# Scores in four row groups per batch, one PSUM ring of seven banks, maxima moved by halves, and a new order of steps, in a two-block transformer kernel

## The reference

```
per attention:  xn = layernorm(x) (* (1 + scale) + shift)
                q, k, v = xn or context @ weights (+ bias)        # second block: rotary on q and k
                attn = softmax(q @ k.T / sqrt(8)) @ v             # 16 heads
                x = x + (gate *) (attn @ W_o + b_o)
per MLP:        x = x + (gate *) (gelu(norm(x) @ W1 + b1) @ W2 + b2)
```

## Time and profile before

| what | value |
| --- | --- |
| median of 3 runs (lowest to highest) | 484.12 us (484.04 to 486.06) |
| the profiled execution | 484.91 us |
| its span in the profile | 483.0 us |
| mean granted TensorE clock | 0.954 of full |
| PE busy | 409.0 us (85%) |
| DVE busy | 327.5 us (68%) |
| ACT busy | 268.2 us (56%) |
| POOL busy | 160.4 us (33%) |
| chain that ended last | PE 57%, DVE 15%, ACT 11%, issue 7%, POOL 7% |

### The profile page before, as it was taken

One profiled execution on the slowest core, in us unless ns is written; L12 is line 12 of the kernel. 1 busy time (PEld: TensorE's weight loads), 2 busy tenths in 40 slices (PEclk: granted clock), 3 DMA queues, 4 the chain that ended last, 5 costly groups with the idle time before them and its releaser, 6 DMA issues.

```text
span 483.0 us, 10203 instructions
## 1 busy us (share of the span) xinstructions
PE 409.0 (85%) x3872; PEld 252.5 (52%) x3872; DVE 327.5 (68%) x842; ACT 268.2 (56%) x505; POOL 160.4 (33%) x147
## 2 busy tenths in 40 slices
PE   3595869697989879889889799789899999998696
PEld 2343445464656544454454454465565655657464
DVE  5484757759597873783874875899999998431331
ACT  1211645465556647546556566556666667677452
POOL 6728515151616160160160160153251634020130
PEclk9856999989899999999999999999999999999899
DMA  8933021120312120300300400303123030400001
GB/s 249 324 97 123 12 91 45 63 73 24 107 41 92 61 71 4 103 28 2 131 3 2 132 5 0 132 6 130 57 76 108 25 128 4 142 12 24 2 1 43
DMA packets 19399, 33.52 MB, mean 69 GB/s; under 512 B 3871, under 2 KB 8479, under 8 KB 19103
## 3 DMA queue, kind: packets, MB, share of 16 engines
q1 hardware_dynamic: 18903, 32.79, 20.8%
q10 hardware_dynamic: 448, 0.08, 0.1%
HBM read 6.51 MB, written 1.05 MB: 16 GB/s over the span
## 4 chain that ended last, share of the span: by engine, by line
PE 57%; DVE 15%; ACT 11%; issue 7%; POOL 7%; SPq 2%; DMA 1%; ACTq 0%; DVEq 0%; POOLq 0%
PE ps_ao L1025 9%; PE ps_sc L1008 7%; PE ps_misc L916 7%; PE ps_misc L964 7%; DVE maxima L711 6%; PE ps_misc L1052 5%; PE ps_misc L1073 5%; PE ps_misc L986 4%; ACT PT L885 4%; POOL Kd L790 4%; PE ps_misc L921 4%; PE ps_misc L1059 3%; ACT xnT L871 3%; PE ps_misc L973 2%; PE ps_misc L1034 2%
## 5 line engine op out<-in xcount | busy, mean ns | idle before, releaser
L885 ACT ACTIVATE PT<-ps_sc 128x512 f32<-128x512 f32 (+1 forms) x256 | 138.8, 596 | 95.1 <-PE ps_sc L1008 94.4
L711 DVE TENSOR_REDUCE maxima<-ps_misc 128x4 f32<-128x512 f32 (+1 forms) x256 | 154.1, 666 | 33.0 <-PE ps_misc L986 32.8
L790 POOL TENSOR_SCALAR Kd<-Kh,head_rows 128x512 fp32r<-128x512 f32 (+1 forms) x64 | 100.3, 1582 | 132.0 <-ACT Kh L843 79.1
L1008 PE MATMUL ps_sc<-Qd,Ks 64*128 64x256 f32 (+1 forms) x512 | 64.7, 331 | 20.6 <-ACT PT L885 12.2
L1025 PE MATMUL ps_ao<-PT,V 120*18 120x128 f32 (+1 forms) x2048 | 71.8, 281 | 2.8 <-ACT PT L885 2.7
L1008 PEld LDWEIGHTS ps_sc<-Qd,Ks 64*128 64x128 f32 (+1 forms) x512 | 37.8, 183 | 57.2 <-issue 34.2
L771 POOL TENSOR_SCALAR vareps<-mv 128x4 f32<-128x4 f32 (+1 forms) x28 | 6.7, 240 | 168.2 <-DVE mv L605 167.6
L1025 PEld LDWEIGHTS ps_ao<-PT,V 120*18 120x18 f32 (+1 forms) x2048 | 51.3, 99 | 17.9 <-issue 6.2
L916 PE MATMUL ps_misc<-cst 128*128 128x384 f32 x128 | 55.8, 552 | 1.8 <-DVE att L725 1.6
L986 PE MATMUL ps_misc<-Kd,Qh 32*128 32x512 f32 (+1 forms) x256 | 44.9, 522 | 12.6 <-POOL Kd L790 8.3
L871 ACT ACTIVATE xnT<-ps_misc,vec 128x128 f32<-128x128 f32 x80 | 30.1, 457 | 40.6 <-PE ps_misc L921 40.6
(11 more groups left out here) (80 smaller groups left out, 474.7 us busy)
## 6 DMA issues: line engine op xcount, KB each, us to landing
Qd<-Qh SPq DMA_DIRECT2D x64, 128.0 KB, 2.6
Qd<-Ql SPq DMA_DIRECT2D x32, 128.0 KB, 2.6
Ks<-Kh SPq DMA_DIRECT2D x32, 128.0 KB, 2.6
Ks<-Kh SPq DMA_DIRECT2D x32, 120.0 KB, 2.6
Ks<-Kl SPq DMA_DIRECT2D x16, 128.0 KB, 2.6
Ks<-Kl SPq DMA_DIRECT2D x16, 120.0 KB, 2.6
W<-weights SPq DMA_DIRECT2D x1, 1792.0 KB, 16.8
x<-x_in SPq DMA_DIRECT2D x4, 256.0 KB, 5.9
```

Of the source, the lines that this page charges most:

```text
L711: dve.tensor_reduce(maxima[:, c, :, st.b], bank(st.use + c)[:, 0:NG * ns].rearrange("p (n k) -> p n k", n=NG), AX_X, ALU.max, negate=True) ...
L790: pool.tensor_scalar(Kd[:, st.f % 2, st.h, 0:n], f32(Kh[:, st.f % 2, 0:n]), head_rows[:, st.h:st.h + 1], None, ALU.mult).then_inc(S["kd_re ...
L885: act.activation(PT[0:ns, st.k % PSLOTS, g, :, :, :].rearrange("p i e t -> p (i e t)"), ps_sc[0:ns, g, :], ACT.Exp, scale=SCALE).then_inc( ...
L1008: ins = pe.matmul(ps_sc[0:ns, side, i * E * P:(i + 1) * E * P], Ks[rows, st.f % 2, n, st.b * ns:(st.b + 1) * ns], Qd[rows, st.f % 2, :, n, ...
```

## The change

What it does, part by part:

- A `score` step is one batch. Each of 16 matmuls has 32 rows and 128 columns; four consecutive ones go to the four row groups and to four banks. `Qd` loses its dimension of two and with it the zero halves; each key or query move is one DMA of 256 KB in place of two of 128 KB.
- `ps_sc` is gone. Scores use four banks of the one ring, which has seven. ScalarE takes four exponentials per step. `PT` holds three batches in place of four half batches.
- The maxima are transposed, copied and moved in two halves of two batches; the first scores wait for the first half only. `values` of two batches fill `ps_ao` before a `copy`, as before in number.
- `warm` matmuls stand in front of `norm` and `aT` (one each, 384 columns), and no longer in front of `xT`, `o`, `h2`, `yT`.
- ScalarE issues the loads of the context, its transpose, the second part of the weights and the bias rows, after its first exponential. The two norms' statistics have semaphores of their own.
- The formula of times is replaced by a table with one pair of times (for `plan` and for `late`) for every step of every unit.

```diff
-BANKS = 5
+BANKS = 7
-PSLOTS = 4
-WARM = {"xT": 2, "o": 1, "h2": 1, "yT": 1}
+PSLOTS = 3
+WARM = {"norm": 3, "aT": 3}
...
-T = dict(
...
-EARLY = [-0.01, -3.59, -1.1, 0.07]
-MLP_LATER = {6: 11.9}
+TIMES = {
...
+    "max": ((23.57, 24.98, 27.38, 30.38, 32.77, 46.21, 50.26, 53.8, 61.91, 67.66, 69.68, 73.68, 83.46, 89.21,
...
+    "score": ((35.18, 36.51, 39.03, 41.28, 57.78, 59.84, 63.84, 65.65, 79.13, 81.39, 85.39, 87.2, 100.68, 102.97,
...
+    "mT": ((29.18, 33.98, 50.74, 58.28, 71.17, 79.63, 92.72, 101.18, 113.88, 121.9, 135.2, 140.25, 153.17,
...
+        elif st.kind == "mods":
+            uses.append(("vec_ready", NV))
+        elif st.kind == "score":
+            uses += [("probs_ready", HG * st.k + c + 1) for c in range(HG)]
...
-        Qd = sb("Qd", [P, 2, E, NG, CT], F32R)
+        Qd = sb("Qd", [P, 2, NG, CT], F32R)
-        maxima = sb("maxima", [P, HG, NG, CB])
-        maxT = sb("maxT", [H * CB, P], F32R)
-        PT = sb("PT", [P, PSLOTS, GP, GP, E, P])
+        maxima = sb("maxima", [P, 2, HB, HG, NG])
+        maxT = sb("maxT", [H * HB, 2, P], F32R)
+        PT = sb("PT", [P, PSLOTS, HG, NG, P])
...
-        ps_sc = ctx.enter_context(nc.psum_tensor("ps_sc", [P, 2, CT], F32))
...
                         for part in (0, 1) if high else (2,):
-                            for e in range(E):
-                                sp.dma_start(f32(Ks[ROW * e + part:P:E * ROW, st.f % 2, :, 0:n]),
-                                             f32(src[HALF * e:HALF * (e + 1), st.f % 2, 0:n])
-                                             ).then_inc(S[f"keys_in{st.f % 2}"], 16)
+                            sp.dma_start(f32(Ks[part:P:ROW, st.f % 2, :, 0:n]),
+                                         f32(src[:, st.f % 2, 0:n])).then_inc(S[f"keys_in{st.f % 2}"], 16)
...
+                        for b in range(HB):
+                            at = (HB * st.h + b) * P
+                            sp.dma_start(f32(Qd[SPLIT:P:TROWS, st.f % 2, :, at:at + P]),
+                                         f32(maxT[H * b:H * (b + 1), st.h, :])
+                                         ).then_inc(S[f"maxima_in{st.f % 2}_{st.h}"], 16)
...
+                act.wait_ge(S["small_in"], 48)
+                act.activation(silu[:, 0, :], condT, ACT.Exp, scale=-1.0).then_inc(S["exp_done"], 1)
                 for c in range(HG):
                     act.dma_start(bias_qk[TROWS * c:TROWS * c + TROWS, :],
                                   by_rows(biases[:, BIAS["q0"]:BIAS["k1"] + 1], c)).then_inc(S["bias_in"], 16)
+                act.dma_start(craw[0:NS_CTX, :, :, :].rearrange("p s b f -> p (s b f)"),
+                              ctx_in).then_inc(S["ctx_in"], 16)
+                act.dma_start(W[:, W_SECOND - W_FIRST:W_TOTAL - W_FIRST],
+                              weights[:, W_SECOND:W_TOTAL]).then_inc(S["rest_in"], 16)
...
                     elif st.kind == "score":
...
-                        for g in range(GP):
-                            act.wait_ge(S[f"scores_ready{g}"], st.k + 1)
-                            act.activation(PT[0:ns, st.k % PSLOTS, g, :, :, :].rearrange("p i e t -> p (i e t)"),
-                                           ps_sc[0:ns, g, :], ACT.Exp, scale=SCALE).then_inc(S["probs_ready"], 1)
+                        act.wait_ge(S["misc_filled"], st.use + HG)
+                        for c in range(HG):
+                            act.activation(PT[0:ns, st.k % PSLOTS, c, :, :].rearrange("p n t -> p (n t)"),
+                                           bank(st.use + c)[0:ns, :], ACT.Exp,
+                                           scale=SCALE).then_inc(S["probs_ready"], 1)
...
-                        for i in range(GP):
-                            n = GP * st.g + i
-                            for side in range(GP):
-                                rows = slice(HALF * side, HALF * (side + 1))
-                                ins = pe.matmul(ps_sc[0:ns, side, i * E * P:(i + 1) * E * P],
+                        if st.b % HB == 0:
+                            pe.wait_ge(S[f"maxima_in{st.f % 2}_{st.b // HB}"], 16 * HB * (st.f // 2 + 1))
+                        for n in range(NG):
+                            for c in range(HG):
+                                rows = slice(TROWS * c, TROWS * c + TROWS)
+                                if n == 0:
+                                    fill(st.use + c)
+                                ins = pe.matmul(bank(st.use + c)[0:ns, n * P:(n + 1) * P],
                                                 Ks[rows, st.f % 2, n, st.b * ns:(st.b + 1) * ns],
-                                                Qd[rows, st.f % 2, :, n, st.b * P:(st.b + 1) * P],
+                                                Qd[rows, st.f % 2, n, st.b * P:(st.b + 1) * P],
                                                 start=True, stop=True)
```

More of the change, by code:

```diff
@@ L194, in make_plan, with at @@
 def make_plan():
     steps = []
[L203 to L210, removed]
+    def at(name, number, st):
+        when, late = TIMES[name]
+        steps.append((when[number], len(steps), st))
+        st.late = late[number], len(steps)
     for f in range(len(ATTN) * STREAMS):
-        a, s, t = f // STREAMS, f % STREAMS, period * f
+        a, s = f // STREAMS, f % STREAMS
@@ L223, in make_plan @@
[L223 to L230, removed]
+            at("cstats", s, Step("cstats", **who))
+            at("cln", s, Step("cln", **who))
@@ L244, in make_plan @@
-        at(t + period + T["aT"][a], Step("aT", **who))
+            at("max", CB * f + b, Step("max", b=b, **who))
+            at("score", CB * f + b, Step("score", b=b, **who))
+            at("value", CB * f + b, Step("value", b=b, **who))
+        for h in range(2):
+            for kind in ("mT", "mmove", "copy", "norm"):
+                at(kind, 2 * f + h, Step(kind, h=h, **who))
+        at("aT", f, Step("aT", **who))
         if ATTN[a]["gate"] is None:
             if ATTN[a]["bias"]:
-                at(t + T["bias"][a], Step("bias", **who))
-            at(t + period + T["o"][a], Step("out", **who))
-        else:
-            at(t + period + T["o"][a], Step("o", **who))
-            at(t + period + T["yT"][a], Step("yT", **who))
+                at("bias", s, Step("bias", **who))
+            at("out", f - STREAMS, Step("out", **who))
+        else:
+            at("o", s, Step("o", **who))
+            at("yT", s, Step("yT", **who))
@@ L270, in make_plan @@
+    at("mods", 0, Step("mods"))
     plan = [st for _, _, st in sorted(steps, key=lambda x: x[:2])]
-    rest = Step("mods")
-    rest.late = [st for st in plan if st.kind == "q" and st.f == 0][0].late
-    plan.insert([st.kind for st in plan].index("q") + 1, rest)
     for s in range(STREAMS):
@@ L445, in block_kernel, with scored @@
         GROUPS = NG * CB
-        MOVES = 16 * E * SPLIT
-        def scored(engine, pairs):
-            for g in range(GP):
-                engine.wait_ge(S[f"scores_ready{g}"], pairs)
+        MOVES = 16 * SPLIT
+        def scored(engine, units):
+            engine.wait_ge(S["probs_ready"], HG * CB * units)
         def bank(n):
@@ L913, in warm @@
                 def warm(st):
-                    for _ in range(WARM[st.kind]):
-                        pe.matmul(bank(st.use)[:, 0:3 * P], ident, ident[:, None, :].to_broadcast([P, 3, P]),
+                    n = WARM.get(st.kind, 0)
+                    if n:
+                        pe.matmul(bank(st.use)[:, 0:n * P], ident, ident[:, None, :].to_broadcast([P, n, P]),
                                   start=True, stop=True)
```

325 lines of the change are left out of this document (210 added, 115 removed), and 54 rows, old and new, of the table TIMES.

## The result

The changed kernel takes 449.61 us (median of four runs, 447.26 to 450.05) against 484.21 us (484.04 to 486.06). The ratio of the two is 0.926, 95% interval 0.923 to 0.929: 34.6 us less. On another chip the same kernel took 449.33 us, ratio 0.925 (0.921 to 0.929). 449.61 us is inside the stated range of 418 to 456 and outside the likeliest case's own range of 421 to 442: between the forecast of 431 and the rival of the coupled ring, 461.

A forecast was written before the change was run, and what follows sets the result against it. PE with its waits was taken as the bound, with DVE in D and chains of short steps in the front and F. Gains of front and stretches summed to 42.5 to 63.7, taken as 54: 484.9 - 54 = 431 us, range 418 to 456.

The forecast's parts named there:

- the rival of the coupled ring: Scores and maxima share one ring, so in-order PE waits for VectorE and densities fall five points: 461 us, 17 in 100.
- Scores in four row groups: Score steps on PE: a batch takes 0.44 us, saving 0.43 a batch, 27.5 us over 64 batches.
- Ring: Shared PSUM banks: a score may wait behind a reduction; costed from no gain in PE's busy share to 0.914.
- My own sign of being wrong: Wrong if PE waits on reductions or exponentials before filling banks for more than some 20 us in all.
- Warming: Matmuls on PE that keep the clock up: 48 in place of 64, 14.0 us less PE work.
- A: Stretch from 46.0 to 144.6 us before, scores of units 0 to 3: gain 11.2 to 18.7 us.
- the clock rival: The granted clock falls and PE's work at 1.2 GHz takes twice as long, 60 us more: 491 us, 4 in 100.
- Front: Start of the kernel, 0 to 46.0 us before: first score at 35.5, 10.5 us earlier, bounds 8 and 12.
- B and C: Stretches 144.6 to 200.0 and to 303.3 us before, units 4 to 8: gains 7.2 to 8.5 and 13.8 to 17.2 us.
- D and E: Stretches 303.3 to 390.0 and to 440.1 us before, units 9 to 14: gains 0 to 2.2 and 1.3 to 2.1 us.
- F: Last stretch, after 440.1 us before, a chain from x through statistics to MLP: gain 1 to 3 us.
- Moves, halves, and ScalarE's loads: Key and query transfers, maxima by halves and ScalarE's load issues: moves covered, loads and halved zeroing taken as 0.

The follow-up runs named there:

- the cut of the maxima: The changed kernel with each maxima reduction reading only half of its columns and the exponentials' scale cut to an eighth: 429.77 us, ratio 0.887.
- doubled scores: The changed kernel with the 16 score matmuls of every batch issued twice: about 471 us, ratio to before 0.9716.
- six banks: The changed kernel with six banks in the ring instead of seven, the order of steps not placed anew: 480.29 us, ratio 0.988.
- half exponentials: The changed kernel with each exponential taking half of its columns, the other probabilities staying at one: 432.16 us, ratio 0.890.

## Why the prediction came out as it did

Right in sign and within the range; too optimistic by 18.6 us in the likeliest case. Point by point:

- **What bounds the kernel**: right for TensorE (four fifths of added work show), but incomplete. Half the columns of the maxima gave 12.5 us in the kernel before, and I had read VectorE's 0.57 to 0.75 of busy time as room everywhere but in D. A page of shares doesn't show this. The waits of TensorE's loads for reductions do: 9.8 us before, 16.5 after. My sum also took PE's busy time as work, and the cut of the maxima took 15 us off it without taking a matmul away.
- **Scores in four row groups**: the mechanism is right (loads side by side), the size is not. A batch takes 0.57 and not 0.44 us of TensorE. Over 64 batches that is an estimated 8.3 us of work more, some 7 by the slope of the doubled scores. The sentence that failed is "the `max` step has the same 512 columns": it has them behind one load a row group, a batch of scores behind four.
- **Ring**: I costed it "within the densities below: from no gain at all in density to that of D". That a full ring could hold TensorE inside a score step had no number. It had 33 gaps, 18.1 us, against 0.7 before, of which the pitch of a round itself is about 4: some 13 us net. My own sign of being wrong, over 20 us of waits on reductions or exponentials for a bank, came true with 34.2, although that is hardly more than the 31.8 of the two kinds of banks before: the change moved these waits and did not remove them. The rival of the coupled ring (461) named the mechanism and set it too high.
- **Warming**: the term "14.0 us less" counted work and got the amount right (41.4 us now). What it is worth in time was wrong: in the kernel before the same edit costs 8 us. I had treated warming as load alone in the sum and the clock only as a rival that begins in A. The falls came elsewhere, in C, D and E. They are short, and A's did not spread, so the clock rival (491) did not come; but the 21.8 us more behind the front are up to 11 us of time, for which the sum had nothing.
- **The 18.6 us in all**: longer batches (7), gaps in the ring (13), the clock (up to 11) and the front (4.2) make more than that. They overlap, and no run separates them, so how the miss divides stays open.
- **Front**: 6.3 instead of 10.5. I let the maxima of unit 0 start at 22.8 as before. The table puts the projections of unit 1 ahead of them, and at the lower clock four of these matmuls took 3.78 us (1.99 before); so the maxima began at 28.48. From there the sum is as foreseen: VectorE reduces without a break, 20 in 12.05 us, and the first exponential is at 40.53, when it ends. (The first matmul of a score starts at 38.58.) With six banks, with doubled scores and with half exponentials the same projections took 1.98 us, the maxima began at 25.27 to 26.14, and the front ended at 37.3 to 39.0. So 2 to 3 of the 4.2 us missing here are the clock of this execution, which is luck, and the rest is the order.
- **A**: 3.9 instead of 15, the largest miss. Its PE busy time did not fall (83.9 against 82.3), where I had 73. Some 4 us of this are projections that stood in B before. It has the in-step gaps, the longer batches and 18 us at the lower level as before; I cannot split the rest among them. Its units are 21.7 to 25.9 us apart, where I had 21; those of C, at 28.9 to 30.5, came as foreseen.
- **B and C**: 26.7 against 23.4, at a PE share of 0.967 in C, above the 0.914 that I thought best; the surplus is the work that went to A. From A to C together it is 30.6 against 38.4. **D and E**: 0.4 against 2.8, with VectorE at 0.88 of D. This looks right by luck: an MLP of 7.5 us left for F, and 17 us at the lower level came, where before there was none.
- **F**: 1.8 longer, not 2 shorter. PE is busy 36.7 us there against 33.0: it has three MLPs where two stood. From D to F together it is 1.4 longer, not 4.8 shorter.
- **Moves, halves, and ScalarE's loads** at nothing: borne out. A 256 KB move lands in 2.6 us, and the scores' 8.2 us wait for moved maxima is down to 0.8 us. The loads were worth up to 2.5, not 0 (intervals overlap).

## What to carry to other kernels

Removing work from the busiest engine pays only as far as its queue isn't held by something else: add up the waits of TensorE's loads for the readers of its banks, and try one PSUM bank less before counting on a shared ring. When matmuls are cut into shorter ones, measure the pitch of a whole step, not only the columns. An ablation that gains time may have gained it through the clock: compare the time at the lower level of both profiles, and stretches that the cut cannot touch. Matmuls that only keep the clock up are not work to be saved: measure them by taking them out of the kernel before.

## What the runs showed of the hardware that was not expected

Sixteen loads and matmuls of 32 rows and 128 columns, four row groups at a time, start in rounds 0.106 us apart after the first, but the batch as a whole holds TensorE for 0.57 us when other work follows (0.47 before another batch, seen once). One bank of PSUM less in a ring of seven cost some 30 us of 450, in an order made for seven. Without any warming matmul the lower clock level held for 106 us of 459, and 41 us less TensorE work made the kernel 9 us slower.
